# Weighted sums of two groups formed together, and transposed maxima kept behind the scores, in a two-layer cross-attention kernel

## What is computed

```python
# layer 0: 8 heads of 40; the last 4 context tokens are kept apart (ca)
hs  = mha(x @ Wq, enc @ Wk, enc @ Wv)              # 371 keys
hs1 = mha(ca_q1, x, x)                             # 112 keys, queries made from ca
hs2 = mha(hs1 @ Wq, ca @ Wk_ca, ca @ Wv_ca)        # 4 keys
x1  = (hs + hs2) @ Wout + b_out + x
# layer 1: 20 heads of 16, 375 keys
out = mha(x1 @ Wq, ctx @ Wk, ctx @ Wv) @ Wo + bo + x1
```

## Time and profile before

| | |
|---|---|
| time, median of 3 runs | 767.23 us (765.45 to 767.73) |
| the profiled execution | 766.16 us |
| its span, first to last instruction | 764.4 us |
| PE (TensorE matmul) | 707.8 us busy, 6916 matmuls |
| DVE (VectorE) | 472.7 us busy |
| ACT (ScalarE) | 403.6 us busy |
| POOL (GpSimd) | 294.3 us busy |
| mean granted TensorE clock | 0.981 |

### The profile page before, as it was taken

One profiled execution on the slowest core, in us unless ns is written; L12 is line 12 of the kernel. 1 busy time (PEld: TensorE's weight loads), 2 busy tenths in 40 slices (PEclk: granted clock), 3 DMA queues, 4 the chain that ended last, 5 costly groups with the idle time before them and its releaser, 6 DMA issues. The chain is left out here.

```text
span 764.4 us, 18175 instructions
## 1 busy us (share of the span) xinstructions
PE 707.8 (93%) x6916; PEld 614.1 (80%) x6916; DVE 472.7 (62%) x1028; ACT 403.6 (53%) x923; POOL 294.3 (39%) x401
## 2 busy tenths in 40 slices
PE   6878899999999999999999999999999999999975
PEld 4667788888888888888888888888888888888763
DVE  1554475757666575756666575766657575666662
ACT  1455365555555555556555555555555555654432
POOL 5387444414244443515344441524444250530300
PEclk9979999999999999999999999999999999999997
DMA  9433534352615334251524335262433425051400
GB/s 322 140 124 80 125 85 93 81 114 60 139 58 126 75 100 92 64 138 47 135 74 104 76 84 118 59 138 59 122 64 106 94 71 138 16 137 31 85 2 15
DMA packets 52387, 72.45 MB, mean 95 GB/s; under 512 B 12128, under 2 KB 44256, under 8 KB 52304
## 3 DMA queue, kind: packets, MB, share of 16 engines
q1 hardware_dynamic: 44832, 60.34, 31.1%
q0 software_dynamic: 6144, 9.25, 6.4%
q10 hardware_dynamic: 1328, 1.71, 0.6%
HBM read 20.60 MB, written 4.26 MB: 33 GB/s over the span
## 5 line engine op out<-in xcount | busy, mean ns | idle before, releaser
L768 DVE TENSOR_REDUCE negmax<-bankS 112x2 f32<-112x750 f32 (+1 forms) x224 | 208.7, 932 | 59.4 <-PE bankS L1147 32.7
L492 POOL DMA_DIRECT2D k_stack<-stage x192 | 96.2, 509 | 137.6 <-DVE stage L804 120.0
L572 ACT ACTIVATE arena<-bankST 125x1344 f32<-125x1344 f32 x80 | 103.4, 1293 | 31.8 <-PE bankST L1181 31.8
L1213 PE MATMUL bankO<-arena,v 125*32 125x112 f32 (+2 forms) x2688 | 107.9, 265 | 6.2 <-ACT arena L572 4.6
L1213 PEld LDWEIGHTS bankO<-arena,v 125*32 125x32 f32 (+2 forms) x2688 | 81.7, 118 | 29.0 <-issue 12.7
L472 POOL TENSOR_TENSOR x1b<-x,bias_sb 112x320 f32<-112x320 f32 x16 | 13.8, 863 | 232.5 <-DMA out<-x1b 204.9
L1147 PE MATMUL bankS<-k_stack,q1T 112*112 112x376 f32 x320 | 87.7, 355 | 3.5 <-DVE negmax L768 3.0
L993 PE MATMUL bankX<-ctx_hi,WH 128*120 128x376 f32 (+2 forms) x192 | 70.3, 366 | 0.8 <-DVE qn L760 0.3
L993 PE MATMUL bankX<-WH,ctx_hi 128*125 128x320 f32 x192 | 66.2, 345 | 0.0
L1181 PE MATMUL bankST<-q1T,k_stack 112*125 112x224 f32 x480 | 65.7, 272 | 0.3 <-DMA q1T<-mT 0.3
L993 PE MATMUL bankX<-ctx_hi,WL 128*120 128x376 f32 (+2 forms) x192 | 65.5, 341 | 0.0
(11 more groups left out here) (139 smaller groups left out, 1535.0 us busy)
## 6 DMA issues: line engine op xcount, KB each, us to landing
k_stack<-stage SPq DMA_DIRECT2D x96, 176.2 KB
k_stack<-stage SPq DMA_DIRECT2D x192, 70.5 KB, 2.6
k_stack<-stage POOLq DMA_DIRECT2D x192, 47.0 KB, 2.0
ctx_raw<-in_ctxT SPq DMA_DIRECT2D x16, 376.0 KB, 3.3
k_stack<-stage SPq DMA_DIRECT2D x48, 117.5 KB
xp<-in_xpad SPq DMA_DIRECT2D x16, 224.0 KB, 3.4
x_raw<-in_xT SPq DMA_DIRECT2D x16, 168.0 KB, 2.3
out<-x1b SPq DMA_DIRECT2D x16, 140.0 KB, 2.8
```

What stands on the lines that cost most here:

```text
L492: pool.dma_start(dst, src).then_inc(k1_stacked_pool[b % 2], 16)
L572: nc.scalar.activation(dst[0:KC], bankST[0:KC, :, 0:GROUP * SQ], ACT.Exp).then_inc(exp_done, 1)
L768: nc.vector.tensor_reduce(negmax[:, n % 2, 2 * pair:2 * pair + 2], bankS[0:SQ, :, 0:keys], axis=AX, op=ALU.max, negate=True).then_inc(max_ ...
L1213: last = nc.tensor.matmul(dst, v, src[0:keys, c, SQ * j:SQ * j + SQ], start=(c == 0), stop=(c == NKC - 1))
```

## The change

`attend` and `copy_o` take a list of one or two groups, an episode. In an iteration there are four: both groups of layer 0 (in slot 3, where the second one had its sums before), groups 0 and 1 of layer 1 (slot 5), 2 and 3 (slot 0), and 4 alone (slot 1). Slots 2, 4 and 6 have no weighted sums. Layer 0's four column blocks lie side by side in `bankO`, in columns 0 to 447; a layer-1 episode uses columns 224 to 447. `pv_done` and `o_copied` count episodes.

The transposed maxima move from `bankO` to the second bank of `bankS`, columns 384 to 495, behind the scores. For this the transpose waits for the slot's first maximum, which reads that bank, and the second matmul of a score pair, which writes that bank, waits until the maxima have been copied. The transpose's wait for the copy of the sums and the sums' wait for the copy of the maxima are gone.

```diff
+EPISODES = [e for b in range(B + 1) for e in
+            ([[(0, b, 0), (0, b, 1)]] if b < B else []) +
+            ([[(1, b - 1, 0), (1, b - 1, 1)], [(1, b - 1, 2), (1, b - 1, 3)], [(1, b - 1, 4)]] if b > 0 else [])]
+EPISODE = {g: n for n, e in enumerate(EPISODES) for g in e}
+
+def attended_at(t, i):
+    late = scored_at(t, i, LAG)
+    return EPISODES[EPISODE[late]] if late and EPISODES[EPISODE[late]][-1] == late else None
...
-        bank_mT = bankO[0:GROUP, 0:SQ]
+        bank_mT = bankS[0:GROUP, 1, SKP + 8:SKP + 8 + SQ]
...
                 if n >= 2:
-                    act.wait_ge(pv_done, n - 1)
+                    act.wait_ge(pv_done, EPISODE[GROUPS[n - 2]] + 1)
...
-            def copy_o(g):
-                layer, b, k = g
-                n = NUMBER[g]
-                dve.wait_ge(pv_done, n + 1)
+            def copy_o(groups):
+                layer, b, k = groups[0]
+                dve.wait_ge(pv_done, EPISODE[groups[0]] + 1)
                 if layer == 0:
-                    dst, src = o0T[:, 2 * k:2 * k + 2, :].rearrange("p c q -> p (c q)"), bankO[:, 0:2 * SQ]
+                    dst, src = o0T[:, :, :], bankO[:, 0:4 * SQ]
                 else:
-                    at = (2 + n % 2) * SQ
-                    dst, src = o1T[:, k, :], bankO[:, at:at + SQ]
+                    dst, src = o1T[:, k:k + len(groups), :], bankO[:, 2 * SQ:(2 + len(groups)) * SQ]
...
                 for j in range(2):
                     h = GROUP * k + 2 * pair + j
+                    if j == 1 and transposed > 0:
+                        pe.wait_ge(mT_copied, transposed)
...
-            def transpose_m(g, attended):
+            def transpose_m(g, scoring):
                 n = NUMBER[g]
-                pe.wait_ge(max_done, 2 * n + 2)
+                if scoring:
+                    pe.wait_ge(max_done, 2 * NUMBER[scoring] + 1)
+                else:
+                    pe.wait_ge(max_done, 2 * n + 2)
                 if n > 0:
                     pe.wait_ge(mT_copied, n)
-                else:
-                    pe.wait_ge(g_split, 4)
-                if attended > 0:
-                    pe.wait_ge(o_copied, attended)
...
-            def attend(g, transposed):
-                pe.wait_ge(exp_done, n + 1)
-                pe.wait_ge(mT_copied, transposed)
+            def attend(groups):
+                n = EPISODE[groups[0]]
                 if n > 0:
                     pe.wait_ge(o_copied, n)
+                else:
+                    pe.wait_ge(g_split, 4)
+                for g in groups:
+                    layer, b, k = g
+                    pe.wait_ge(exp_done, NUMBER[g] + 1)
...
                 last.then_inc(pv_done, 1)
...
-                    if late:
-                        attend(late, transposed)
-                        attended = NUMBER[late] + 1
+                    if attended_at(t, i):
+                        attend(attended_at(t, i))
```

More of the change, by code:

```diff
@@ L625, in unit @@
                     elif i == 0:
-                        act.wait_ge(pv_done, NUMBER[0, b - 1, 1] + 1)
+                        act.wait_ge(pv_done, EPISODE[0, b - 1, 1] + 1)
                     nc.scalar.activation(v0[0:KC, i, :].rearrange("p (h d) -> p h d", h=H0)[:, :, 0:D0],
@@ L633, in unit @@
                     elif i == 0:
-                        act.wait_ge(pv_done, NUMBER[1, b - 2, G1 - 1] + 1)
+                        act.wait_ge(pv_done, EPISODE[1, b - 2, G1 - 1] + 1)
                     nc.scalar.activation(v1[b % 2][0:KC, i, :].rearrange("p (h d) -> p h d", h=H1)[:, :, 0:D1],
@@ L774, in copy_mT @@
                 nc.vector.tensor_copy(mT[:, n % MT_BUFS, :], bank_mT).then_inc(mT_copied, 1)
[L776 to L779 removed]
+            def copy_o(groups):
+                layer, b, k = groups[0]
+                dve.wait_ge(pv_done, EPISODE[groups[0]] + 1)
                 if layer == 0:
[L781 removed]
+                    dst, src = o0T[:, :, :], bankO[:, 0:4 * SQ]
                 else:
[L783 to L784 removed]
+                    dst, src = o1T[:, k:k + len(groups), :], bankO[:, 2 * SQ:(2 + len(groups)) * SQ]
+                dst = dst.rearrange("p c q -> p (c q)")
                 nc.vector.tensor_copy(dst, src).then_inc(o_copied, 1)
@@ L906, in _ @@
                 for i in range(SLOTS):
-                    g, before, late = scored_at(t, i), scored_at(t, i, 1), scored_at(t, i, LAG)
+                    g, before = scored_at(t, i), scored_at(t, i, 1)
                     if g:
@@ L923, in _ @@
                         unit(*u)
-                    if late:
-                        copy_o(late)
+                    if attended_at(t, i):
+                        copy_o(attended_at(t, i))
                     for u in units_of(t, i, 3):
@@ L1078, in unit @@
                     layer, k = {"N0": (0, 1), "N1a": (1, 3), "N1b": (1, 4)}[kind]
-                    pe.wait_ge(o_copied, NUMBER[layer, b, k] + 1)
+                    pe.wait_ge(o_copied, EPISODE[layer, b, k] + 1)
                     cols = [o0T[:, c, :] for c in range(4)] if layer == 0 else [
@@ L1123, in unit, with scores @@
                 last.then_inc(unit_filled, 1)
-            def scores(g, pair):
+            def scores(g, pair, transposed):
                 layer, b, k = g
@@ L1185, in shifted_scores @@
                 last.then_inc(st_done, 1)
-            def attend(g, transposed):
-                layer, b, k = g
-                n = NUMBER[g]
-                pe.wait_ge(exp_done, n + 1)
-                pe.wait_ge(mT_copied, transposed)
+            def attend(groups):
+                n = EPISODE[groups[0]]
                 if n > 0:
                     pe.wait_ge(o_copied, n)
[L1194 to L1199, removed]
-                else:
-                    at_once = [(c, j) for c in range(NKC) for j in range(GROUP)]
-                for c, j in at_once:
-                    h = GROUP * k + j
+                else:
+                    pe.wait_ge(g_split, 4)
+                for g in groups:
+                    layer, b, k = g
+                    pe.wait_ge(exp_done, NUMBER[g] + 1)
+                    if k == 0:
+                        for i in range(NKC):
+                            pe.wait_ge(bank_drained[bank(f"V{layer}_{i}", b)], drained(f"V{layer}_{i}", b))
+                    src = PT[:, NUMBER[g] % 2]
@@ L1213, in attend @@
-                    last = nc.tensor.matmul(dst, v, src[0:keys, c, SQ * j:SQ * j + SQ], start=(c == 0),
-                                            stop=(c == NKC - 1))
+                        at_once = [(c, j) for pair in range(2) for c in range(NKC) for j in (2 * pair, 2 * pair + 1)]
+                    else:
+                        at_once = [(c, j) for c in range(NKC) for j in range(GROUP)]
+                    for c, j in at_once:
+                        h = GROUP * k + j
+                        if layer == 0:
+                            keys = KC if c < 2 else KC - NTOK
+                            at = (2 * k + j // 2) * SQ
+                            dst = bankO[64 * (j % 2):64 * (j % 2) + 64, at:at + SQ]
+                            v = v0[0:keys, c, 64 * h:64 * h + 64]
+                        else:
+                            keys = KC
+                            at = (2 + k % 2) * SQ
+                            dst = bankO[32 * j:32 * j + 32, at:at + SQ]
+                            v = v1[b % 2][0:keys, c, 32 * h:32 * h + 32]
+                        last = nc.tensor.matmul(dst, v, src[0:keys, c, SQ * j:SQ * j + SQ], start=(c == 0),
+                                                stop=(c == NKC - 1))
@@ L1230, in _ @@
             unit("S2_1", 0)
-            attended = transposed = 0
+            transposed = 0
             for t in ITERATIONS:
@@ L1236, in _ @@
                     if g:
-                        scores(g, 0)
+                        scores(g, 0, transposed)
                     for u in units_of(t, i, 0):
@@ L1242, in _ @@
                     if before:
-                        transpose_m(before, attended)
+                        transpose_m(before, g)
                         transposed = NUMBER[before] + 1
@@ L1247, in _ @@
                     if g:
-                        scores(g, 1)
+                        scores(g, 1, transposed)
                     for u in units_of(t, i, 2):
                         unit(*u)
-                    if late:
-                        attend(late, transposed)
-                        attended = NUMBER[late] + 1
+                    if attended_at(t, i):
+                        attend(attended_at(t, i))
                     for u in units_of(t, i, 3):
```

7 lines of the change are left out of this document (removed).

## The result

The changed kernel takes 832.61 us (median of 4 runs, 820.57 to 838.3) against 767.48 us for the kernel before beside it. The ratio counts only the two faster of the four runs (820.57 and 830.28 us) and is 1.0755, 95% interval 1.0638 to 1.0873. The forecast was 792, with 801 as the upper end. The direction was right, the size was not: 65 us between the medians (58 by the ratio) instead of 25. The profiled execution took 830.28 us, with a span of 828.4.

What follows compares the result with a forecast made beforehand. TensorE, busy 707.8 us or 93% of the span, was taken to bound the kernel. 15.2 + 0.7 - 1 + 10.4 = 25.3 us on 766.16 gave 791.5, put at 792; range 779 to 801.

Steps and rivals of the forecast that it cites:

- slot 3, paid again: Slot 3: the 24 matmuls moved from slot 2 add 1.17 us per iteration in full, 13 times, 15.2 us.
- layer-1 joins: Slots 4 to 0: each join saves 0.20 us, twice per iteration, but q0's wait for x_hi hides it; taken as 0.
- new waits in the loop: Slot 3: the second score matmul waits for VectorE's copy of the maxima, 0.05 x 13 = 0.7 us; elsewhere hidden.
- clock behind slot 2: After slot 2's 1.69 us stall TensorE's clock halves in 8 of 13 iterations, 1.3 us each: 10.4 us, bounds 0 and 19.5.
- ends: Iterations 0, 1, 15 and 16, where the steady loop's pattern does not hold: -1 us together, between -4 and +2.
- Slot 2, gain 0: Slot 2: S2_1 still starts 2.68 us after S2_0, held by ScalarE's exponentials; PE idles 1.69 us instead of 0.33.
- x_hi chain: K0_2's drain, SyncE's stacking DMAs and output store, GpSimd's x_hi, then q0: 24.9 us, beginning behind slot 3.
- some 0.4 us each in five slots: Iteration 16: the two new waits make PE and VectorE take turns, copy 0.26 us and two latencies each.
- That rival: The clock stays up: same slot 2 stall but no slow stretches, 781 us; chance 0.22.
- Faster by shape changes: All 48 removed visits give 0.20 us each, 9.6 us, if slot 2 exposes less than 0.20: 756.5 us; chance 0.10.
- Partly covered: Slot 3's 1.17 us displaces N0's 0.52 idle, returning 6.8 us, clock up: 774; chance 0.04 including nothing.
- New waits in full: The second wait's 0.6 us and slot 4's 0.4 are not hidden, 13 us on top: 805 us; chance 0.06.

Runs made afterwards that it cites:

- the filler: The full change plus seven unused 448-column matmuls in slot 2 between N1b and S2_1, iterations 2 to 14: 799.94 us, 1.0436 to the kernel before.
- bank-only kernel: The kernel before with no groups joined, only the transposed maxima moved behind the scores with their two waits: 773.58 us, ratio 1.0086.
- the early store: The kernel before with SyncE's store of the result issued ahead of the 12 stacking DMAs: 761.57 us, ratio 0.9921.

## Why the prediction was wrong in size

The forecast's terms against what the parts show. The loop is 12 of the 13 iterations with a stall; the 13th is in the tail, where by the loop's means it stands for about 1.1 us in slot 3 and 3.4 of clock (estimates).

| term | forecast, us | measured, us |
|---|---|---|
| slot 3, paid again | 15.2 | about 14 (13.1 in the loop) |
| layer-1 joins | 0 | 0 in the loop |
| new waits in the loop | 0.7 | 0.4 |
| clock behind slot 2 | 10.4 | about 38 (34.3 in the loop) |
| ends | -1 | about +12 |
| sum | 25.3 | 64 |

Two stretches of the kernel before, at half the clock, belong beside the table's row on the clock; the earlier trace rows and the forecast's sum do not have their lengths:

```profile
36.20:46.40 10.20, 6.62 (x26) 5.54 (x27) 6.84 (x8) 5.36 (x15) 7.55 (x6) 0.50 0.36 129
...
753.00:764.40 11.40, 5.84 (x40) 4.32 (x40) 2.42 (x8) 0.59 (x3) 0.00 (x0) 0.50 0.04 13
```

- **Slot 2, gain 0: right.** S2_0 to S2_1 is 2.68 or 2.69 us in all 13 iterations, and S2_1's wait is 22.0 us, the 13 x 1.7 that was named. Taking 22 matmuls out of the same place in the kernel before gained nothing either.
- **Slot 3, +1.17 us each: right.** The visit grew by 2.46 - 1.31 = 1.15 us. With the filler, an iteration costs 13.1 / 12 = 1.09 more.
- **Layer-1 joins, 0.20 us each but hidden: right, and shown from both sides.** They gained nothing with the x_hi chain in place (773.47 us with them and 773.58 without in the new bank, 1.0046 [1.0015, 1.0077] in the old one) and 0.39 us per iteration without it. Their small cost in the old bank was not forecast.
- **The two new waits: right in the loop, wrong at the end.** The loop's 0.4 us is the bank-only kernel's. The term "some 0.4 us each in five slots" found the wait (1.6 us in six times, 0.4 at most), but I let it be cancelled inside the estimate for the ends.
- **The clock: this is the step that failed,** in size and not in kind. The step was "I take 8 of the 13, at 1.3 us". It was 11 of 13, and each fall in the loop cost 34.3 / 10 = 3.4 us. The frequency is a small part of the miss. The larger one is the length: I took the 3.4 us of one fall in the head as the length of any fall, and even the upper bound of 13 x 1.5 rested on it. The trace of the kernel before already had the two longer ones shown above, 10.2 us in its head and 11.4 us at its end. Most falls behind slot 2 last 6.8 us, some 10.2, and PE is busy nearly all that time (6.80 of 6.80 us at 428.0, 9.51 of 10.20 at 571.4). So hardly any of the slow time falls on a wait, although I had assumed that some of it would.
- **By the rule of the Trainium skill ("TensorE: Matmul & The Clock Gate", "HAM oscillation — how this bites in real kernels")** the clock would have stayed up and the time been 781. The trace decides against that reading: with one idle gap of 1.69 us in slot 2 the clock fell 11 times, and filling the gap removed every fall behind slot 2. That rival fell, and with it the lower end of my range.
- **The ends, "-1 us": wrong, the second miss.** The head grew by 5.8 us and the layer-0 join alone does it: the head is 142.5, 142.6 and 145.0 us in the three traces with it, and at most 139.4 in those without. I had counted the removed visit of iterations 0 and 1 as a gain. In the changed kernel the low clock from 56.0 lasts 10.2 us where it lasted 3.4 us, and that from 80.6 has become one of 6.8 us; so the head is thin already, and thinning it further costs clock. That this is the whole cause was not tested by a filler there. Of the tail's 10.8 us some 4.5 belong to the 13th iteration and 5.3 to the new bank; the last 1.0 is not assigned.
- **The other rivals.** "Faster by shape changes" fell at its own condition: slot 2 exposed 1.69 - 0.33 = 1.36 us more, not under 0.20. "Partly covered" fell too: N0's old cover is now the transpose's wait, and it moved along. "New waits in full" had a loss near the right size for a cause that is not there in the loop.

## What to carry to other kernels

Work that stands between a producer and its late consumer costs nothing where it is; before moving it, read which chain sets the distance, and price it where it goes. Then ask what TensorE's clock will do with the hole, and price a fall by the longest ones that the trace shows, not by the shortest: here the clock cost more than twice what the moved work did. And a saving behind another chain is worth having only together with the edit that shortens that chain, as with the early store.

## What was not expected of the hardware

- **More work, less time.** Seven useless 448-column matmuls in a 1.69 us hole, 1.66 us of PE time per iteration, took the loop from 571.4 to 538.8 us. Removing 22 of 24 matmuls from the same place in the kernel before lengthened it from 524.0 to 540.3.
- **The same slot, two outcomes.** Around the stall, from 379.0 and from 423.25, PE is busy 1.71 of 3.40 and 1.68 of 3.37 us, with the same 1.69 us of idle time. After the first the clock stays at 1.00, after the second it is at 0.50 from 428.0. With holes of 1.32 us (less work) it fell in four of twelve loop iterations, with 1.69 us in ten of twelve (the change) and twelve of twelve (layer 0 joined alone). Behind q0's waits it was the same: it fell once after 1.81 us (filler) and once after 1.56 (layer 1 joined, old bank), and it stayed up after 1.93 (the change) and after 1.47 and 1.51 (layer 1 joined, new bank). What picks the iteration is not settled by these runs.
- **A fall outlasts its cause.** Behind slot 2 PE is busy with hardly a break (73.4 us of the 74.8 us that the eleven falls last), yet the clock came back only after 3.4, 6.8 or 10.2 us.
- **Two visits less, 0.20 us each.** From the pair of kernels with the early store: a removed separate visit of 32-row weighted sums is worth 0.20 us on the path, as the earlier trace rows had said.
